# Attention kernel on one core: second weight halves, batch 1's normalisation and the last outputs in another order and on other engines

## The chip, the cores and the metric

The kernel runs on one core of a Trainium2 chip. The time is device microseconds (us) of the whole program on that core; it ran three times: 1285.94, 1286.47 and 1288.19 us, median 1286.47. Five engines work side by side, each through its own list of instructions in order: TensorE (PE; its weight loads are PEld), VectorE (DVE), ScalarE (ACT), GpSimd (POOL) and SyncE (SP, which issues the transfers). They wait for one another on semaphores.

## The reference

```python
def _layernorm(x, axis=-1, eps=1e-05):
    m = jnp.mean(x, axis=axis, keepdims=True)
    v = jnp.var(x, axis=axis, keepdims=True)
    return (x - m) / jnp.sqrt(v + eps)
# x: (32, 256, 512), adj: (32, 256, 256), W*: (512, 512), float32; 16 heads, hd = 32
h = jnp.maximum(_layernorm(x, axis=-1), 0.0)
q = split_heads(h @ Wq.T); k = split_heads(h @ Wk.T); v = split_heads(h @ Wv.T)
a = jnp.einsum('bhnd,bhmd->bhnm', q, k) * D ** (-0.5) + (adj + adj)[:, None]
row_nonzero = jnp.any(a != 0, axis=-1, keepdims=True)
a = jnp.where(row_nonzero, a, -jnp.inf)
p = jax.nn.softmax(a, axis=-1)
p = jnp.where(jnp.isnan(p), 0.0, p)
o = jnp.einsum('bhnm,bhmd->bhnd', p, v)
return x + o.transpose(0, 2, 1, 3).reshape(B, N, D) @ Wo.T
```

## The kernel before

Nearly every matrix is split into a high and a low part, so that a float32 product is made of three products (high by high, high by low, low by high) into one PSUM bank. A value is split in two steps: ACT copies it from PSUM into the high part, then DVE subtracts that from PSUM and writes the low part.

**Weights.** Wq, Wk and Wv arrive as six halves in the order `TURNS` (Wq 0, Wk 0, Wq 1, Wk 1, Wv 0, Wv 1). Of each half: its extent (DVE `weight_extent`, or ACT `sum_weight`), three small DVE instructions that make a scale (`weight_scales`), a multiplication by it in place (ACT for Wq 0, `scale_first_weight`; POOL for the other five, `scale_weight`, L929), eight transposes on PE (`turn`, L431), and the split (`high_weight` on ACT, `low_weight` on DVE). Half 0 of Wq and Wk is all that the products qk 0 and qk 1 (heads 0 to 7) read; half 1 serves qk 2 and qk 3.

**A batch.** POOL's `normalise` (L863) writes h from x and the moments that DVE's `moments_of` made; PE transposes it (job h); jobs qk and v are its products with the weights; SP restacks the parts of q and k for the scores by twelve transfers for each eight heads (`stack`, L242). Then for each of 16 heads: `scores` on PE, `shift` on DVE (adds 2 adj, takes the bound of each row), `exponentials` on ACT, `transpose_probs` on PE, `high_probs` on ACT and `low_probs` on DVE, `values` on PE. For each pair of heads POOL folds the rows to see whether one is all zero (`fold`), DVE makes the row factors (`any_nonzero`, `factors`), ACT copies the sums out of PSUM (`copy_outputs`) and POOL adds their halves and multiplies by the factors (`divide`, L884). Job o transposes eight heads' outputs, job y multiplies them by Wo, ACT copies y out of PSUM and POOL adds x (`residual`, L898).

**What sets the order.** A table, `JOBS`, says which pieces of which job PE does in which head's slot, and for which batch (-1, 0 or 1 from the present one). `body(b, first, last)` writes out one batch on each engine; batches 1 to 30 are a hardware loop, 0 and 31 are written out apart. Ahead of body 0 stand the instructions of the weights and of batch 0's first products; behind body 31 those that finish its outputs: `values` of heads 14 and 15, job o 1 (heads 8 to 15 together, into the bank `s_ps0`), and the second halves of y 0 and y 1 (L496 to L500). Their first halves stand in the slot of head 15, by `LAST_JOBS`, so ahead of the values of heads 14 and 15.

Of the kernel before, what the change touches and what calls it, by code (L numbers as in the profile page):

```python
# [47 lines left out]
LAST_JOBS = {15: [("y", 0, 0, 0, 6), ("y", 1, 0, 0, 6)]}  # L48


# [11 lines left out]
def jobs_at(hh, first, last):  # L62

    here = [j for j in JOBS[hh] if not (first and j[2] < 0) and not (last and j[2] > 0)]
    return here + (LAST_JOBS.get(hh, []) if last else [])

# [10 lines left out]
def attention_block(nc, x, adj, wq, wk, wv, wo_t, out):  # L77
# [23 lines left out]
    with ExitStack() as ctx:  # L101
# [102 lines left out]
        o_copied, y_ready = sem("o_copied"), sem("y_ready")  # L204
        stored = [sem(f"stored{i}") for i in range(NT)]
# [14 lines left out]
        def bank(kind, n, b):  # L220
# [4 lines left out]
            if isinstance(b, int) and (kind, n, b) == ("o", 1, B - 1):  # L225
                return 2
# [14 lines left out]
        def _(sp):  # L241
# [65 lines left out]
            for t in range(NT):  # L307
                store(B - 1, t)
# [4 lines left out]
        def _(pe):  # L313
# [140 lines left out]
            turn(WQ, 1)  # L454
# [40 lines left out]
            body(B - 1, False, True)  # L495
            for hh in range(HEADS - 2, HEADS):  # L496
                values(B - 1, hh, False)
            job("o", 1, -1, 0, 4, B)
            for n in range(NT):
                job("y", n, -1, 6, 12, B)  # L500

        @block.scalar
        def _(act):
# [105 lines left out]
            sum_weight(WQ, 1)  # L609
# [4 lines left out]
            high_weight(WQ, 1)  # L614
# [5 lines left out]
            high_weight(WK, 1)  # L620
            high_weight(WV, 0)
            high_weight(WV, 1)
            copy_adj(0)
            take("v", 0, 0, True)
            exponentials(0, 0, True)
# [28 lines left out]
            copy_outputs(B - 1, PAIRS - 1, False)  # L654
            take("o", 1, B - 1)
            for n in range(NT):
                take("y", n, B - 1)

        @block.vector
        def _(dve):  # L660
# [144 lines left out]
            weight_scales(WQ, 1)  # L805
            weight_scales(WK, 1)
# [12 lines left out]
            low_weight(WK, 1)  # L819
            low_weight(WV, 0)  # L820
            low_weight(WV, 1)
            take("v", 0, 0)
            shift(0, 0, True)
            take("qk", 2, 0)
            shift(0, 1, True)
# [29 lines left out]
        def _(pool):  # L855
# [93 lines left out]
            for half in range(2):  # L949
                scale_out_weight(half)  # L950
# [55 lines left out]
```

## Time and profile before

| | us |
|---|---|
| median of three runs | 1286.47 |
| the profiled execution, whole | 1286.69 |
| its span, first to last instruction | 1284.9 |
| PE busy in the span | 1246.0 (97%) |
| DVE busy | 1111.5 (87%) |
| ACT busy | 1052.2 (82%) |
| POOL busy | 898.3 (70%) |

The profile divides the span into busy time of each engine; a busy PE is not PE at its peak. Times in rows count from the span's start. The `<-` in brackets at the end of a row names what ended the engine's idle time before it.

### The profile page before, as it was taken

The page shows a single profiled execution, that of the slowest core. Times are in us where ns is not written, and L with a number is a line of the kernel's source. Part 1 is how long each engine was busy: PE and PEld are TensorE (multiplying, and loading weights), DVE is VectorE, ACT ScalarE, POOL GpSimd, SP SyncE. Part 2 cuts the span into 40 slices and gives each one's busy share as a digit, 9 for nine tenths or more (in the row PEclk, how much of TensorE's full clock was granted, in tenths as well). Part 3 has the DMA queues.
Part 4 walks back from the last instruction along what each step waited for, and adds up shares of the span by engine and source line. Part 5 has one row for each costly group of instructions (what it writes and reads, how often), then busy time and mean ns, then how long its engine had stood idle before and what let it go on. Part 6 is the DMA issues. An engine that isn't in the chain of part 4 may idle for free. (4 is left out here: it accounts for less than half of the span.)

```text
span 1284.9 us, 43970 instructions
## 1 busy us (share of the span) xinstructions
PE 1246.0 (97%) x13104; PEld 1110.2 (86%) x13104; DVE 1111.5 (87%) x4003; ACT 1052.2 (82%) x2429; POOL 898.3 (70%) x1272
## 2 busy tenths in 40 slices
PE   4899999999999999999999999999999999999996
PEld 4788988888988888888888888888888888988885
DVE  5798888888888888888888888888889898889884
ACT  4788888888888888888888888888888888888884
POOL 6676677776677776677776677776677776677765
PEclk9999999999999999999999999999999999999998
DMA  6344554554554554554554554554554554554551
GB/s 216 96 110 126 135 123 126 135 143 112 137 122 124 137 140 113 139 122 122 139 134 117 141 122 120 141 132 116 144 122 117 144 131 115 147 122 115 130 123 51
DMA packets 90772, 163.88 MB, mean 128 GB/s; under 512 B 14976, under 2 KB 23168, under 8 KB 90752
## 3 DMA queue, kind: packets, MB, share of 16 engines
q1 hardware_dynamic: 90752, 163.64, 49.1%
q8 instruction: 10, 0.16, 0.1%
q14 instruction: 10, 0.08, 0.0%
HBM read 46.14 MB, written 16.78 MB: 49 GB/s over the span
## 5 line engine op out<-in xcount | busy, mean ns | idle before, releaser
L912 POOL TENSOR_TENSOR fold<-minus 128x512 f32<-128x512 f32 x256 | 326.9, 1277 | 299.2 <-DVE bounds L765 299.2
L586 ACT ACTIVATE probs<-minus,bounds 128x256 f32<-128x256 f32 x1024 | 459.8, 499 | 26.6 <-DVE bounds L765 25.0
L774 DVE TENSOR_TENSOR pT_lo<-pT_ps,pT_hi 128x512 f16<-128x512 f32 x512 | 351.2, 686 | 63.2 <-ACT pT_hi L597 60.0
L765 DVE CUSTOM_DVE_ANT_0 minus<-s_ps,adj_now 128x256 f32<-128x256 f32 x1024 | 388.6, 416 | 7.7 <-ACT probs L586 4.7
L597 ACT ACTIVATE pT_hi<-pT_ps 128x512 f16<-128x512 f32 x512 | 304.9, 596 | 109.6 <-PE pT_ps L406 107.9
L406 PE MATMUL pT_ps<-ident,probs 128*128 128x128 f32 x2048 | 307.5, 273 | 1.7 <-ACT probs L586 1.6
L331 PE MATMUL job_ps<-hT_hi,w_hi 128*128 128x256 f16 x1024 | 280.5, 274 | 0.8 <-DVE hT_lo L729 0.8
L331 PE MATMUL job_ps<-hT_hi,w_lo 128*128 128x256 f16 x1024 | 279.2, 273 | 0.0
L331 PE MATMUL job_ps<-hT_lo,w_hi 128*128 128x256 f16 x1024 | 279.1, 273 | 0.0
L406 PEld LDWEIGHTS pT_ps<-ident,probs 128*128 128x128 f32 x2048 | 241.8, 141 | 19.0 <-ACT probs L586 2.5
L395 PE MATMUL s_ps<-qk_stack 96*128 96x256 f32 x1024 | 246.8, 323 | 0.0
L918 POOL TENSOR_TENSOR bounds<-fold 128x256 f32<-128x256 f32 x256 | 187.8, 734 | 24.9 <-POOL fold L912 9.5
L427 PE MATMUL o_ps<-v_parts,pT_hi 128*128 128x65 f16 x2048 | 157.1, 192 | 8.2 <-DVE pT_lo L774 7.7
L395 PEld LDWEIGHTS s_ps<-qk_stack 96*128 96x128 f32 x1024 | 154.6, 191 | 0.3 <-DMA qk_stack<-qk_parts 0.2
L428 PE MATMUL o_ps<-v_parts,pT_lo 128*128 128x33 f16 x2048 | 150.2, 178 | 0.0
L427 PEld LDWEIGHTS o_ps<-v_parts,pT_hi 128*128 128x128 f16 x2048 | 123.8, 97 | 24.0 <-DVE pT_lo L774 11.6
L331 PE MATMUL job_ps<-w_hi,hT_hi 128*128 128x256 f16 x512 | 140.7, 275 | 1.8 <-DVE qk_parts L737 1.8
L331 PE MATMUL job_ps<-w_lo,hT_hi 128*128 128x256 f16 x512 | 139.8, 273 | 0.0
L331 PE MATMUL job_ps<-w_hi,hT_lo 128*128 128x256 f16 x512 | 139.6, 273 | 0.0
L428 PEld LDWEIGHTS o_ps<-v_parts,pT_lo 128*128 128x128 f16 x2048 | 126.8, 96 | 0.0
L892 POOL TENSOR_TENSOR o<-o_raw,factor 128x128 f32<-128x128 f32 x256 | 103.1, 403 | 20.1
L331 PEld LDWEIGHTS job_ps<-hT_hi,w_hi 128*128 128x128 f16 x1024 | 99.8, 97 | 16.0 <-issue 0.9
(79 smaller groups left out, 2264.3 us busy)
## 6 DMA issues: line engine op xcount, KB each, us to landing
qk_stack<-qk_parts SPq DMA_DIRECT2D x768, 128.0 KB, 2.3
x_in<-x SPq DMA_DIRECT2D x32, 512.0 KB, 3.4
x_res<-x SPq DMA_DIRECT2D x32, 512.0 KB, 3.7
out<-y SPq DMA_DIRECT2D x64, 256.0 KB, 2.1
adj_in<-adj SPq DMA_DIRECT2D x32, 256.0 KB, 3.5
w_in<-wq SPq DMA_DIRECT2D x2, 512.0 KB, 6.1
w_in<-wk SPq DMA_DIRECT2D x2, 512.0 KB, 7.9
w_in<-wv SPq DMA_DIRECT2D x2, 512.0 KB, 9.9
```

What stands on the lines that cost most here:

```text
L331: end = nc.tensor.matmul(dst, lhs[a](k), rhs[c](k), start=i == 0, stop=i == len(terms) - 1)
L395: end = nc.tensor.matmul(s_ps[SCORE_BANK[hh]][:, t * N:(t + 1) * N], stack[:, 0, t * P:(t + 1) * P], stack[:, 1, :], start=True, stop=True)
L406: end = nc.tensor.transpose(pT_ps[hh % 2][:, m * N + t * P:m * N + (t + 1) * P], probs[hh % 2][:, t, m * P:(m + 1) * P], ident[:, :])
L427: nc.tensor.matmul(ps[:, 0:LOW + HD], hi, v[:, 0:LOW + HD], start=m == 0, stop=False)
L428: end = nc.tensor.matmul(ps[:, 0:HD + 1], lo, v[:, 0:HD + 1], start=False, stop=m == NT - 1)
L586: end = nc.scalar.activation(probs[hh % 2][:, t, :], minus[hh // 2 % 2][:, hh % 2, t, :], ACT.Exp, bias=bounds[:, hh // 2 % 4, 2 * (hh % 2 ...
L597: nc.scalar.activation(pT_hi[hh % 4][:, :, :], pT_ps[hh % 2][:, :].rearrange("p (m n) -> p m n", m=NT), ACT.Copy).then_inc(pT_high, 1)
L765: end = nc.vector.tensor_tensor_reduce(out=minus[pair % 2][:, hh % 2, t, :], in0=s_ps[SCORE_BANK[hh]][:, t * N:(t + 1) * N], in1=adj_now[: ...
L774: nc.vector.tensor_tensor(pT_lo[hh % 4][:, :, :], pT_ps[hh % 2][:, :].rearrange("p (m n) -> p m n", m=NT), pT_hi[hh % 4][:, :, :], ALU.sub ...
L892: nc.gpsimd.tensor_tensor(o[:, :, col:col + 2 * HD].rearrange("p t (h d) -> p h t d", h=2), o_raw[pair % 2][:, :, 0:HD].rearrange("p (h t) ...
L912: nc.gpsimd.tensor_tensor(f1[:, :, :], src[:, :, 0:N // 2], src[:, :, N // 2:N], ALU.add).then_inc(folded1, 1)
L918: nc.gpsimd.tensor_tensor(f2, f1[:, :, 0:N // 4], f1[:, :, N // 4:N // 2], ALU.add).then_inc(folded2, 1)
```

## The change

**Ahead of body 0.** PE does qk 0 and qk 1 before it turns Wq 1; Wk 1, Wv 0 and Wv 1 follow. ACT sums Wq 1 only after it has made the high part of Wk 0, and ACT and DVE split the four second halves after qk 1 is taken. The score products of heads 0 and 1 move one job forward. The multiplication of the weights on POOL gets a second operand, 1.0, with a second multiplication. DVE makes the moments of batch 1 and POOL normalises it there, and body 0 no longer does.

**Behind body 31.** `LAST_JOBS` goes. Heads 8 to 11 (k = 2) are transposed and split by themselves right behind head 15's transposes, heads 12 to 15 (k = 3) at the end; PE takes y in pieces of six, three and three products with the values of heads 14 and 15 after the first six. The last pair's sums are copied, added and multiplied by DVE, not by ACT and POOL, and the last residual is one DVE addition out of PSUM in place of an ACT copy and a POOL addition. The loop of batches 1 to 30 keeps its instructions.

```diff
-LAST_JOBS = {15: [("y", 0, 0, 0, 6), ("y", 1, 0, 0, 6)]}
@@ PE, ahead of body 0
             turn(WK, 0)
-            turn(WQ, 1)
             weight_waits(pe, WQ, 0)
             job("qk", 0, 0, 0, 12, 0)
             weight_waits(pe, WK, 0)
             job("qk", 0, 0, 12, 24, 0)
             job("qk", 1, 0, 0, 24, 0)
+            turn(WQ, 1)
             turn(WK, 1)
             turn(WV, 0)
             turn(WV, 1)
             weight_waits(pe, WV, 0)
+            scores(0, 0, True)
             job("v", 0, 0, 0, 12, 0)
-            scores(0, 0, True)
+            scores(0, 1, True)
             job("qk", 2, 0, 0, 24, 0)
-            scores(0, 1, True)
             job("v", 1, 0, 0, 12, 0)
@@ PE, behind body 31
+            def last_turn(k):
+                if k == 2:
+                    pe.wait_ge(o_ready, (B - 1) * PAIRS + 6)
+                else:
+                    pe.wait_ge(o_ready, (B - 1) * PAIRS + 7)
+                    pe.wait_ge(last_o, 1)
+                for t in range(NT):
+                    end = nc.tensor.transpose(s_ps[0][:, (k % 2) * N + t * P:(k % 2) * N + (t + 1) * P],
+                                              o[:, t, k * P:(k + 1) * P], ident[:, :])
+                end.then_inc(last_turned, 1)
...
+            last_turn(2)
+            last_product(0, 0, 6)
             for hh in range(HEADS - 2, HEADS):
                 values(B - 1, hh, False)
-            job("o", 1, -1, 0, 4, B)
-            for n in range(NT):
-                job("y", n, -1, 6, 12, B)
+            last_product(1, 0, 6)
+            last_product(0, 6, 9)
+            last_turn(3)
+            last_product(1, 6, 9)
+            last_product(0, 9, 12)
+            last_product(1, 9, 12)
@@ ACT, ahead of body 0
             scale_first_weight()
-            sum_weight(WQ, 1)
             high_weight(WQ, 0)
             for n in range(2):
                 take("h", n, 0)
             high_weight(WK, 0)
-            high_weight(WQ, 1)
+            sum_weight(WQ, 1)
             sum_weight(WV, 0)
@@ ACT, behind body 31
-            copy_outputs(B - 1, PAIRS - 1, False)
-            take("o", 1, B - 1)
-            for n in range(NT):
-                take("y", n, B - 1)
+            for k in range(2, KT):
+                act.wait_ge(last_turned, k - 1)
+                nc.scalar.activation(oT_hi[:, k, :], s_ps[0][:, (k % 2) * N:(k % 2 + 1) * N], ACT.Copy
+                                     ).then_inc(last_high, 1)
@@ DVE, ahead of body 0
             weight_extent(WK, 1)
-            weight_scales(WQ, 1)
-            weight_scales(WK, 1)
             low_weight(WQ, 0)
             for n in range(2):
                 take("h", n, 0)
             low_weight(WK, 0)
-            dve.wait_ge(w_scales, 4)
-            for half in range(2):
-                query_scales(half)
-            low_weight(WQ, 1)
+            dve.wait_ge(w_scales, 2)
+            query_scales(0)
+            weight_scales(WQ, 1)
+            weight_scales(WK, 1)
             take("qk", 0, 0)
...
+            shift(0, 0, True)
             take("v", 0, 0)
-            shift(0, 0, True)
+            shift(0, 1, True)
+            moments_of(1)
             take("qk", 2, 0)
-            shift(0, 1, True)
@@ DVE, behind body 31
+                dve.wait_ge(o_ready, (B - 1) * PAIRS + pair - 1)
+                nc.vector.tensor_copy(o_raw[pair % 2][:, :, 0:HD], o_sums[:, :, 0:HD]).then_inc(last_added, 1)
+                dve.wait_ge(last_added, 1)
+                nc.vector.tensor_tensor(o_raw[pair % 2][:, :, 0:HD], o_sums[:, :, LOW:LOW + HD],
+                                        o_raw[pair % 2][:, :, 0:HD], ALU.add).then_inc(last_added, 1)
...
+                nc.vector.tensor_tensor(y[:, t, :], job_ps[BANK["y", t]][:, :], x_res[:, t, :], ALU.add
+                                        ).then_inc(last_y, 1)
...
+            last_low(2)
+            last_outputs()
+            last_low(3)
+            for t in range(NT):
+                last_residual(t)
@@ POOL
                     end = nc.gpsimd.tensor_scalar(w_in[i][:, k, :], w_in[i][:, k, :],
-                                                  w_scale[:, i, UNSCALE, k:k + 1], None, ALU.mult)
+                                                  w_scale[:, i, UNSCALE, k:k + 1], 1.0, ALU.mult, ALU.mult)
...
+            normalise(1, False)
             fold(0, 0, True)
...
-                    if not last and hh == 1:
+                    if not (first or last) and hh == 1:
                         normalise(b + 1, False)
...
-            divide(B - 1, PAIRS - 1)
-            for t in range(NT):
-                residual(B - 1, t)
```

The order of PE ahead of body 0, before (w_in0, 1 and 2 are Wq, Wk and Wv; job_ps1 with w_hi0 is qk 0; s_ps2 and o_ps with w_in0 are the second half of Wq):

```order
L444 MATMUL s_ps0<-ident,w_in1 128x128 x4
L444 MATMUL s_ps1<-ident,w_in1 128x128 x4
L444 MATMUL s_ps2<-ident,w_in0 128x128 x4
L444 MATMUL o_ps<-ident,w_in0 128x128 x4
L331 MATMUL job_ps1<-hT_hi,w_hi0 128x256
L331 MATMUL job_ps1<-hT_lo,w_hi0 128x256
```

and after:

```order
L442 MATMUL s_ps0<-ident,w_in1 128x128 x4
L442 MATMUL s_ps1<-ident,w_in1 128x128 x4
L329 MATMUL job_ps1<-hT_hi,w_hi0 128x256
L329 MATMUL job_ps1<-hT_lo,w_hi0 128x256
...
L329 MATMUL job_ps0<-hT_hi,w_lo1 128x256
L442 MATMUL s_ps2<-ident,w_in0 128x128 x4
L442 MATMUL o_ps<-ident,w_in0 128x128 x4
L442 MATMUL pT_ps0<-ident,w_in1 128x128 x4
```

The eight transposes of Wq's second half have moved from ahead of the first product to behind the 48th. The last rows of DVE, before (pT_lo3 is head 15's low part, some and factor belong to the last pairs):

```order
L774 TENSOR_TENSOR pT_lo3<-pT_ps1,pT_hi3 128x512
L783 TENSOR_REDUCE some1<-bounds 128x4
L787 RECIPROCAL o_ps<-o_ps 128x4
L796 SCALAR_TENSOR_TENSOR factor1<-some1,o_ps 128x4
L747 TENSOR_TENSOR oT_lo<-s_ps0,oT_hi 128x512
```

and after:

```order
L803 TENSOR_TENSOR pT_lo3<-pT_ps1,pT_hi3 128x512
L882 TENSOR_TENSOR oT_lo<-s_ps0,oT_hi 128x256
L890 TENSOR_REDUCE some1<-bounds 128x4
L894 RECIPROCAL o_ps<-o_ps 128x4
L825 SCALAR_TENSOR_TENSOR factor1<-some1,o_ps 128x4
L898 COPY o_raw1<-o_ps 128x4x32
L900 TENSOR_TENSOR o_raw1<-o_ps,o_raw1 128x4x32
L905 TENSOR_TENSOR o<-o_raw1,factor1 128x2x2x32
L882 TENSOR_TENSOR oT_lo<-s_ps0,oT_hi 128x256
L917 TENSOR_TENSOR y<-job_ps1,x_res 128x512
L917 TENSOR_TENSOR y<-job_ps0,x_res 128x512
```

The split of the last transposed outputs has become two halves, and the pair's outputs and both residuals now stand on DVE.

## Rows read from the trace of the kernel before

**Rows 1.** Busy time by stretch: start:end, length, busy of each engine, PEclk, DMA, GB/s.

```profile
24.80:40.60 15.80, 10.37 (x79) 8.81 (x76) 7.25 (x20) 7.34 (x16) 9.27 (x9) 0.89 0.49 117
40.70:60.00 19.30, 16.30 (x175) 14.40 (x174) 16.36 (x60) 15.62 (x37) 14.75 (x19) 1.00 0.45 110
77.00:1263.00 1186.00, 1177.11 (x12509) 1051.30 (x12508) 1052.44 (x3815) 997.16 (x2306) 840.21 (x1199) 1.00 0.50 127
1273.00:1279.20 6.20, 4.79 (x13) 3.58 (x13) 0.69 (x1) 1.19 (x2) 0.18 (x1) 0.50 0.00 0
```

**Rows 2.** Timeline to 20 us: start, length, engine, line, operation, count, idle before.

```profile
11.50 1.22 DVE L677 TENSOR_REDUCE w_scale<-w_in 128x2 f32<-128x1024 f32 x1 [0.79 <-DMA w_in<-wk]
14.72 1.26 DVE L715 TENSOR_TENSOR w_lo<-pT_ps,w_hi 128x512 f16<-128x512 f32 x2
15.91 1.28 DVE L729 SCALAR_TENSOR_TENSOR hT_lo<-job_ps,hT_hi 128x512 f16<-128x512 f32 x2
17.06 1.11 PE L444 MATMUL s_ps<-ident,w_in 128*128 128x128 f32 x4 [1.99 <-POOL w_in L933]
18.82 0.42 PE L331 MATMUL job_ps<-hT_hi,w_hi 128*128 128x256 f16 x1
```

**Rows 3.** POOL's multiplications of weights, by line: ns min/median/max, first and last start.

```profile
L933 POOL TENSOR_SCALAR w_in<-w_in,w_scale x10: 1560/1563/1570, 10.8 to 29.1; 128x512 f32<-128x512 f32 x10
L942 POOL TENSOR_SCALAR wo_in<-wo_in,w_scale x4: 691/692/695, 30.7 to 32.7; 128x512 f32<-128x512 f32 x4
```

**Rows 4.** Timeline, 24 to 40 us.

```profile
24.65 1.04 PE L444 MATMUL pT_ps<-ident,w_in 128*128 128x128 f32 x8
26.03 0.41 DVE L737 SCALAR_TENSOR_TENSOR qk_parts<-job_ps,qk_parts 128x256 fp32r<-128x256 f32 x1
26.53 9.16 SPq L253 DMA_DIRECT2D qk_stack<-qk_parts  x12
30.70 1.12 PE L444 MATMUL s_ps<-ident,w_in 128*128 128x128 f32 x4 [1.99 <-POOL w_in L933]
34.61 0.28 PE L331 MATMUL job_ps<-hT_hi,w_hi 128*128 128x256 f16 x1
37.16 0.48 PE L395 MATMUL s_ps<-qk_stack 96*128 96x256 f32 x2
39.15 0.28 PE L331 MATMUL job_ps<-w_hi,hT_hi 128*128 128x256 f16 x1 [1.51 <-DVE qk_parts L737]
```

**Rows 5.** Transfers by line: count, KB each, median us from issue to landing.

```profile
qk_stack<-qk_parts SPq DMA_DIRECT2D x768, 128.0 KB, 2.3
x_in<-x SPq DMA_DIRECT2D x32, 512.0 KB, 3.4
out<-y SPq DMA_DIRECT2D x64, 256.0 KB, 2.1
```

**Rows 6.** Timeline, body 0 (from 40.7 us).

```profile
43.13 1.27 DVE L665 BATCH_NORM_STATS2 stats<-x_in 128x6 f32<-128x512 f32 x2
45.57 0.91 ACT L586 ACTIVATE probs<-minus,bounds 128x256 f32<-128x256 f32 x2 [1.62 <-PE pT_ps L406]
```

**Rows 7.** Timeline of the end.

```profile
1267.33 0.48 PE L331 MATMUL job_ps<-wo_hi,oT_hi 128*128 128x512 f32 x1 [0.26 <-DVE oT_lo L747]
1268.38 0.68 DVE L774 TENSOR_TENSOR pT_lo<-pT_ps,pT_hi 128x512 f16<-128x512 f32 x1
1270.21 0.20 PE L427 MATMUL o_ps<-v_parts,pT_hi 128*128 128x65 f16 x1
1270.85 0.39 ACT L575 ACTIVATE o_raw<-o_ps 128x260 f32<-128x260 f32 x1 [3.13 <-PE o_ps L428]
1272.73 1.11 PE L371 MATMUL s_ps<-ident,o 128*128 128x128 f32 x4 [1.92 <-POOL o L892]
1275.26 0.79 PE L331 MATMUL job_ps<-wo_hi,oT_hi 128*128 128x512 f32 x1 [1.41 <-DVE oT_lo L747]
1281.02 1.26 POOL L904 TENSOR_TENSOR y<-y,x_res 128x512 f32<-128x512 f32 x1 [0.72 <-ACT y L567]
```

More of the change, by code:

```diff
@@ L62, in jobs_at @@
 def jobs_at(hh, first, last):
-    here = [j for j in JOBS[hh] if not (first and j[2] < 0) and not (last and j[2] > 0)]
-    return here + (LAST_JOBS.get(hh, []) if last else [])
+    return [j for j in JOBS[hh] if not (first and j[2] < 0) and not (last and j[2] > 0)]
 def ended_before(hh, first, last):
@@ L224, in bank @@
                 return 1 - BANK[kind, n]
-            if isinstance(b, int) and (kind, n, b) == ("o", 1, B - 1):
-                return 2
             return BANK[kind, n]
@@ L619, in _ @@
             take("qk", 1, 0, True)
-            high_weight(WK, 1)
-            high_weight(WV, 0)
-            high_weight(WV, 1)
+            for i, half in TURNS[2:]:
+                high_weight(i, half)
             copy_adj(0)
+            exponentials(0, 0, True)
             take("v", 0, 0, True)
-            exponentials(0, 0, True)
             act.wait_ge(q_scales, 2)
@@ L842, in body @@
                     low_probs(b, hh, first and hh < 2)
-                    if not last and hh == 0:
+                    if not (first or last) and hh == 0:
                         moments_of(b + 1)
@@ L849, in _, with last_low, last_outputs @@
             body(B - 1, False, True)
-            any_nonzero(B - 1, PAIRS - 1)
-            factors(B - 1, PAIRS - 1, False)
-            take("o", 1, B - 1)
+            def last_low(k):
+                dve.wait_ge(last_high, k - 1)
+                nc.vector.tensor_tensor(oT_lo[:, k, :], s_ps[0][:, (k % 2) * N:(k % 2 + 1) * N],
+                                        oT_hi[:, k, :].bitcast(F32), ALU.subtract).then_inc(last_taken, 1)
+            def last_outputs():
+                pair = PAIRS - 1
+                dve.wait_ge(folded2, B * PAIRS)
+                nc.vector.tensor_reduce(some[pair % 2][:, :], bounds[:, pair % 4, :, :], AX_X, ALU.max,
+                                        apply_absolute_value=True).then_inc(some_ready, 1)
+                dve.wait_ge(pv_done, B * HEADS)
+                nc.vector.reciprocal(o_sums[:, :, FREE], o_sums[:, :, ONES]).then_inc(rcp_ready, 1)
+                factors(B - 1, pair, False)
+                dve.wait_ge(o_ready, (B - 1) * PAIRS + pair - 1)
[3 more added lines that the diff above has]
+                                        o_raw[pair % 2][:, :, 0:HD], ALU.add).then_inc(last_added, 1)
+                dve.wait_ge(last_added, 2)
+                dve.wait_ge(factor_ready, B * PAIRS)
+                col = 2 * pair * HD
+                nc.vector.tensor_tensor(
+                    o[:, :, col:col + 2 * HD].rearrange("p t (h d) -> p h t d", h=2),
+                    o_raw[pair % 2][:, :, 0:HD].rearrange("p (h t) d -> p h t d", h=2),
+                    factor[pair % 2][:, :].rearrange("p (h t) -> p h t", h=2).unsqueeze(3).to_broadcast([P, 2, NT, HD]),
+                    ALU.mult).then_inc(last_o, 1)
```

29 lines of the change are left out of this document (25 added, 4 removed).

## The prediction

> **What bounds the kernel now.** I read the busy time by stretch first. From 77 to 1263 us PE is busy for 1177.1 of 1186.0 us at a granted clock of 1.00 [rows 1]: 8.9 us of waiting in some 31 batches. The loop is bound by PE and its instructions do not change, so a microsecond won ahead of it moves the whole loop, and one won behind it moves the end. The same view shows where PE is not the bound: 10.4 busy of 15.8 us before body 0, 16.3 of 19.3 us in the first half of body 0, and 4.8 of 6.2 us at clock 0.50 near the end [rows 1]. So I work out three stretches from the timelines: to the first product of v 1, body 0, and the end.
>
> **Up to v 1.** Before, two things hold back the first product (18.82 us). PE stands in the turn of Wq 1, which waits 1.99 us for POOL at 17.06; and DVE, free at 11.50 + 1.22 = 12.72, makes the scales of Wq 1 and Wk 1 until it splits Wq 0 at 14.72 [rows 2]. Both go. ACT's high part of Wq 0 comes earlier too, because its sum of Wq 1 stands behind it now. So DVE's splits move up by 14.72 - 12.7 = 2.0 us, the low part of h ends at 15.91 + 1.28 - 2.0 = 15.2 us, and PE, which has nothing ahead, starts there: 3.6 us earlier. The second twelve products need Wk 0 split, a 1.26 us pair on DVE behind h, so at 16.4; the first twelve last until 16.5. It just fits.
>
> The 48 products of qk 0 and 1 took 24.65 - 18.82 = 5.8 us, the first at 0.42 us each [rows 2, 4]. Twenty-four at full level take 37.16 - 34.61 = 2.55 us [rows 4], so 48 take 5.1. PE will have been busier just before, so I let them run at full level: qk 1 ends at 20.4 instead of 24.65. DVE's take of it ended at 26.03 + 0.41 = 26.44 and the stacking of heads 0 to 7 began at 26.53 [rows 4]; both move up 4.2, to 22.3.
>
> From there DVE splits four second halves, 1.28 us each: Wq 1 by 23.6, Wk 1, then Wv 0 by 26.2, Wv 1 by 27.4. PE turns them at 1.04 to 1.1 us each from 20.4; the turn of Wv 1 uses the bank of Wq 1 and waits for its split, so ends at 24.8, and PE idles for 1.4 us until Wv 0 is split. This is the wait that comes in place of POOL's.
>
> POOL must not be later. Its ten multiplications of weights took 1563 ns each; the four of Wo, of the same 128x512 shape but with two operands and two multiplications, took 692 [rows 3]. The new form is the second one, so I price it at 0.69: Wq 1 can start when its scales are made (about 17.1 us, behind the query scales on DVE), the eight multiplications last 8 x 0.69 = 5.5 us, and with the wait for the scales of Wv they end near 23, ahead of PE's turn. The unknown lies between 0.69 and 1.56 by the rows; I take the lower because the instruction is the same as Wo's. The Trainium skill (GPSIMD Engine Reference, Elementwise, side-by-side cycle accounting) speaks against any gain here: up to two operations per element a body is bound by its ports, so a second multiplication should be free but not negative. The rows have it otherwise, 1563 against 692 ns, and the page's own example of 512 elements, 769 ns, lies by the two-operand rows. By the page read strictly both forms cost the same, and that case is the second rival.
>
> The scores of head 0 need three transfers and those of head 1 six. Twelve issues took 9.16 us, 0.76 each, and one lands in 2.3 us [rows 4, 5]: 22.3 + 1.5 + 2.3 = 26.1 and 22.3 + 3.8 + 2.3 = 28.4. PE: scores 0 at 26.2, v 0 until 27.9, scores 1 at 28.4, qk 2 from 28.7. In the kernel before qk 2 began at 34.61 and v 1, which waits for its bank, at 39.15 [rows 4]; the same 4.5 us give 33.2. DVE has more ahead of that take than before: the shifts of heads 0 and 1 and the moments of batch 1 (1.27 us of statistics and the aggregation [rows 6]), from 27.4 to about 32.3, then 0.9 for the take: also 33.2. Hence v 1 starts at 33.2 instead of 39.15, **5.9 us**. Bounds: 4.3 if the clock is at half level in the first products (+0.7) and in v 0 (+0.9); 6.6 if the waits for transfers and moments vanish.
>
> **Body 0.** DVE's moments stand at 43.13 ahead of head 3's shift, and ACT then waits 1.62 us at 45.57 [rows 6], from where on it is the engine that keeps PE waiting: PE's idle time from 40.7 to 60 us is 19.3 - 16.3 = 3.0 us [rows 1]. With the moments gone ACT is up to 1.6 us ahead. POOL loses its normalisation here and does it ahead of fold 0; the folds wait for DVE anyway. I take **1.2 us**: most of 1.62, less what PE's own work does not give back. Bounds 0 (PE cannot follow) and 3.0 (all its idle time).
>
> **The end.** Head 15's transposes and the first six products of y 0 keep their time (1267.33): two transposes of heads 8 to 11 slip in ahead while PE waits 0.26 us for DVE [rows 7]. Before, twelve products stood until 1270.21 ahead of the values of heads 14 and 15, whose last input was ready at 1268.38 + 0.68 = 1269.06 [rows 7]. Twelve took 2.88 us, so 0.24 each. After: six until 1268.8, the values until 1269.35, six of y 1 until 1270.8, three of y 0 until 1271.5. DVE meanwhile: half of oT low (128x256, 0.41 as in [rows 4]) until 1269.5; reduction, reciprocal and factor, each no larger than that, 0.7 together; copy, addition and multiplication of 128x128. Those three have no row before. From 0.68 for 512 columns and 0.41 for 256 I extrapolate 0.27, with hand-over 0.32 each; bounds 0 and 0.41. The output is ready at 1271.1, in time for the turn at 1271.5; there is 0.4 us to spare, so even 0.41 each costs nothing. Two transposes (0.3), ACT's copy (0.39), DVE's split (0.41) with their hand-overs end at 1272.8, beside three products of y 1 (until 1272.4). PE waits 0.4 us, does the last six products until 1274.35, and DVE's second residual (128x512, 0.68) ends at 1275.1.
>
> Before, the last addition ended at 1281.02 + 1.26 = 1282.28 and the span at 1284.9, 2.6 later. After, the two stores are issued 0.7 us apart instead of 2; 512 KB take 3.4 us against 2.1 for 256 KB [rows 5], so the second can be late by 0 to 0.7; I take 0.3. End at 1275.1 + 2.6 + 0.3 = 1278.0: **6.9 us** won. What went: ACT's copy (0.39) between values and factors, four transposes at 1.11 us and twelve products begun behind a wait, the first 0.79 us long against 0.48 [rows 7], and a 1.26 us addition behind an ACT copy. Bounds: 5.4 (last six products at half level, 0.2 more each, and the store's 0.7), 7.3 (nothing lost).
>
> **Sum.** 5.9 + 1.2 + 6.9 = 14.0. The profiled execution took 1286.69, of which 1284.9 is span; 1286.69 - 14.0 = 1272.7, and as it was 0.2 above the median of the runs shown, I predict 1272.5.
>
> **Rivals.** First, the clock. PE now has waits of 1.3 to 1.7 us at about 14, 25 and 31 us and 0.4 near the end. Before, a wait of 1.99 us was followed by four transposes in 1.11 us, against eight in 1.04 at full level [rows 2, 4], and the stretch to 40.6 us has clock 0.89 [rows 1]. If the shorter waits do the same, 0.7 + 0.9 in front and 6 x 0.2 = 1.2 at the end are lost: 1275.3. Against it: each is shorter than every wait after which the rows show half level. The Trainium skill (TensorE: Matmul & The Clock Gate, What's actually happening) has the throttled level as the default which activity lifts; that agrees with the 0.50 stretch, and it names no gap as short as these.
>
> Second, POOL's form costs 1.56 as before. Then eight multiplications from 17.1 end at 29.6, the turn of Wv 1 is at 29.7 instead of 30.70, and two pairs of scores now stand ahead of qk 2 (0.3 us more): v 1 comes 0.8 earlier, not 5.9. Sum 8.9: 1277.6. Only rows 3 speak against it, strongly.
>
> Third, slower: the loop settles in another rhythm. Ahead of it ACT, DVE and POOL come out of body 0 with other leads over PE. In body 0 that leads to 3.0 us of PE waits in half a batch. If a tenth of this stayed in each of 31 loop batches, 0.6 us each, 18.6 us are lost: 1291.1. It decides from 14.0 / 31 = 0.45 us a batch. Against it: the instructions and semaphores of the loop are the same, and before, PE's waits fell to 0.3 us a batch straight after a far more disturbed body 0.
>
> Fourth, the gains are absorbed: transfers or DVE hold v 1 where it was and the end gains little; within 0.2%, about 1286.
>
> **Numbers.** Forecast 0.78, clock 0.10, POOL's form 0.08, rhythm 0.02, absorbed 0.02. Runs of this kernel can tell 0.2% (2.6 us) from no change; so faster 0.96, same 0.02, slower 0.02. The range goes from the sum of the high bounds, cut where they would all have to hold together (1269.0), to just past the second rival (1278.0).
>
> **What would show it.** POOL's weight multiplications at about 0.69 us; the first qk product near 15.2, the first stacking transfer near 22.3, the first product of v 1 near 33.2; ACT's 1.6 us wait in body 0 gone; as much time in the loop as before, with PE waiting under 10 us in it; at the end, PE at full level with one wait of about 0.4 us and 2.6 to 3.3 us from the last addition to the end. The prediction is wrong if those multiplications stay at 1.56, if clock 0.50 appears before 33 us or in the last 6 us, or if PE's waits in the loop rise by more than a few us.

## The result and the profile after

The changed kernel took 1275.87 us (median of five runs, 1272.42 to 1277.27), the kernel before beside it 1286.22 us (five runs, 1285.45 to 1288.19): ratio 0.9914, interval 0.9902 to 0.9927. It is faster, by 10.4 us in the medians, and the median lies in the range that was forecast (1269.0 to 1278.0). The profiled execution took 1273.81 us with a span of 1272.0; against the 1286.69 of the one before that is 12.9 us, where the steps of the prediction made 14.0.

GpSimd's multiplications, by line (ns min/median/max, first and last start), of the kernel after, beside [rows 3]:

```profile
L1005 POOL TENSOR_SCALAR w_in<-w_in,w_scale x10: 691/692/704, 10.4 to 22.0; 128x512 f32<-128x512 f32 x10
```

The new form costs what the two-operand form of Wo cost. Now the timeline ahead of v 1 of the kernel after (start, length, engine, line; in brackets the idle time before it and what ended it), beside [rows 2, 4]. Read PE's five rows with a bracket first: they are its waits.

```profile
14.91 0.27 PE L329 MATMUL job_ps<-hT_hi,w_hi 128*128 128x256 f16 x1 [1.54 <-DVE hT_lo L758]
...
18.58 0.48 DVE L764 SCALAR_TENSOR_TENSOR qk_parts<-job_ps,q_scale,qk_parts 128x256 fp32r<-128x256 f32 x1 [1.45 <-ACT qk_parts L583]
...
22.04 8.63 SPq L249 DMA_DIRECT2D qk_stack<-qk_parts  x12
...
23.85 0.63 PE L442 MATMUL s_ps<-ident,w_in 128*128 128x128 f32 x4 [0.91 <-DVE w_lo L744]
...
26.15 0.80 PE L393 MATMUL s_ps<-qk_stack 96*128 96x256 f32 x2 [1.23 <-DVE w_lo L744]
...
26.98 0.42 PE L329 MATMUL job_ps<-w_lo,hT_hi 128*128 128x256 f16 x1
...
29.55 0.28 PE L329 MATMUL job_ps<-hT_hi,w_hi 128*128 128x256 f16 x1
...
34.10 0.28 PE L329 MATMUL job_ps<-w_hi,hT_hi 128*128 128x256 f16 x1 [1.75 <-DVE qk_parts L766]
```

Product v 1 starts at 34.10 us, 5.05 us earlier than before. From 26.15 us PE runs at half level: the two scores take 0.80 us, and each product of v 0 takes 0.42 us where the others take 0.27. The busy time by stretch (columns as in rows 1) shows it as a granted clock of 0.66 in 25 to 30 us, after waits of 1.54, 0.91 and 1.23 us, and shows the loop as it was:

```profile
25.00:30.00 5.00, 3.85 (x20) 3.00 (x21) 3.11 (x9) 2.84 (x6) 0.34 (x1) 0.66 0.74 170
71.00:1257.00 1186.00, 1177.02 (x12507) 1051.16 (x12505) 1052.32 (x3814) 996.75 (x2305) 839.71 (x1199) 1.00 0.50 127
```

PE is busy for 1177.02 us of 1186, against 1177.11 [rows 1]. ACT copies adj once in every batch, so these copies are marks in the loop. One mark near its start and the last mark, first of the kernel before and then of the kernel after:

```profile
L606 ACT ACTIVATE adj_now<-adj_in x2: 633/634/634, 110.1 to 148.7; 128x512 f32<-128x512 f32 x2
L606 ACT ACTIVATE adj_now<-adj_in x1: 633/633/633, 1230.0 to 1230.0; 128x512 f32<-128x512 f32 x1
```

```profile
L636 ACT ACTIVATE adj_now<-adj_in x2: 633/633/633, 103.8 to 142.5; 128x512 f32<-128x512 f32 x2
L636 ACT ACTIVATE adj_now<-adj_in x1: 633/633/633, 1224.2 to 1224.2; 128x512 f32<-128x512 f32 x1
```

From 148.7 to 1230.0 it was 1081.3 us, from 142.5 to 1224.2 it is 1081.7. The 6.2 us won by the first mark are 5.05 up to v 1 and 1.2 in body 0, as PE's first product of qk 0 of batch 1 shows, first in the kernel before and then in the kernel after:

```profile
57.06 0.27 PE L331 MATMUL job_ps<-hT_hi,w_hi 128*128 128x256 f16 x1 [0.82 <-DVE hT_lo L729]
```

```profile
50.82 0.27 PE L329 MATMUL job_ps<-hT_hi,w_hi 128*128 128x256 f16 x1 [0.81 <-DVE hT_lo L758]
```

From v 1 to there it was 17.9 us and is 16.7. ACT's wait ahead of `probs` [rows 6] is gone: it came 6.42 us behind v 1, and the same instruction now starts 4.69 us behind v 1, without a bracket.

```profile
38.79 0.90 ACT L616 ACTIVATE probs<-minus,bounds 128x256 f32<-128x256 f32 x2
```

The profile names PE as what ended the old wait. PE's transposes and DVE's shift of head 3 ended there within 0.01 us of each other; that it was the shift shows in the kernel after, where the instruction starts ahead of those transposes.

The end of the kernel after, beside [rows 7]:

```profile
1260.60 0.63 PE L404 MATMUL pT_ps<-ident,probs 128*128 128x128 f32 x4
...
1264.80 0.29 DVE L905 TENSOR_TENSOR o<-o_raw,factor 128x128 f32<-128x128 f32 x1
...
1265.70 0.38 PE L503 MATMUL s_ps<-ident,o 128*128 128x128 f32 x2
...
1267.01 0.50 PE L329 MATMUL job_ps<-wo_hi,oT_hi 128*128 128x512 f32 x1 [0.23 <-DVE oT_lo L882]
...
1267.58 0.39 PE L329 MATMUL job_ps<-wo_hi,oT_lo 128*128 128x512 f32 x1
...
1268.11 1.36 DVE L917 TENSOR_TENSOR y<-job_ps,x_res 128x512 f32<-128x512 f32 x2 [1.15 <-PE job_ps L329]
```

The clock stays at full level (0.39 us a product, where the half-level one in rows 7 took 0.79 with its start). PE has one wait, 0.23 us. From the transposes of head 15 (1260.60) to the end of the span it is 11.4 us; before, where they stand in this row, it was 18.5.

```profile
1266.43 0.64 PE L406 MATMUL pT_ps<-ident,probs 128*128 128x128 f32 x4
```

### The profile page after: what moved, and what is told of

Read it like the earlier page. It is cut to its first block and busy times, and to the rows that moved or that the text cites. A ratio compares the mean times of both kernels' runs of the same rounds, so it can differ in the third digit from the quotient of the medians.

```text
span 1272.0 us, 43970 instructions
## 1 busy us (share of the span) xinstructions
PE 1241.6 (98%) x13104; PEld 1107.2 (87%) x13104; DVE 1112.8 (87%) x4009; ACT 1050.6 (83%) x2427; POOL 886.1 (70%) x1268
## 5 line engine op out<-in xcount | busy, mean ns | idle before, releaser
L329 PEld LDWEIGHTS job_ps<-hT_hi,w_hi 128*128 128x128 f16 x1024 | 99.7, 97 | 17.6 <-issue 2.6
```

Of the source, the lines that this page charges most:

```text
L329: end = nc.tensor.matmul(dst, lhs[a](k), rhs[c](k), start=i == 0, stop=i == len(terms) - 1)
```

## The experiments

Every kernel was timed four or five times, in three sets (1 to 4, 5 to 8, 9 to 12), each with the kernel before beside it. I call the distance between the lowest and the highest run of a kernel its scatter; much of the story hangs on it. The kernel before scatters too: by 4.2, 4.3 and 2.7 us in the nine runs of each set. The code below is shortened; `...` marks what is left out.

**1 and 2. The front alone, the end alone.** The first has everything ahead of body 0 and the old end; the second the reverse.

```diff
@@ e1: the kernel before with
+ front of every engine, the form with 1.0, moments_of(1) and normalise(1) ahead
@@ e2: the kernel before with
+ last_turn, last_product, last_low, last_outputs, last_residual; no LAST_JOBS
```

> The part ahead of body 0 and the moved normalisation alone, the end as before. Theory A (the gains add, each where the prediction put it): 6.2 us off the kernel before (5.05 by the first product of v 1, 1.2 in body 0), so near 1280.0, and in the trace v 1 at 34.1 us. Theory B (what the loop does with its start takes part of it back, the 2 us by which the median of the changed kernel lies above its profiled execution): 4 us off, near 1282.2, with the loop longer by 2 us and v 1 still at 34.1.

> The new end alone, everything ahead of the loop and body 0 as before. Theory A: 7.1 us off the kernel before, near 1279.1, with TensorE at full level to the end. Theory B gives the same 7.1, since the start is the old one. If it is the end that varies between executions (TensorE's level there), the times scatter by 1 to 2 us and the mean gain is 5.5.

Measured: 1280.32 us (1279.77 to 1280.42, ratio 0.9954, interval 0.9940 to 0.9967) and 1279.20 us (1277.46 to 1280.31, ratio 0.9947, interval 0.9933 to 0.9961), before 1285.89. The front is worth 5.6 us and the end 6.7, each by an interval of some 3.5 us in width. Together 12.3; the whole change was worth 11.8 in the same set (next run). The parts add up within what the runs can tell, and the loop took the same: from mark to mark, as above, 1081.5 us in the first and 1081.7 in the second. In the front-only kernel v 0 ran at half level again, and there PE had waited only 0.81, 0.91 and 1.23 us:

```profile
25.00:30.00 5.00, 3.77 (x21) 2.75 (x20) 3.59 (x10) 2.89 (x6) 0.76 (x2) 0.70 0.91 207
```

Two things in these traces warn against trusting one pair of profiles. In the end-only kernel the front is that of the kernel before, and still v 1 comes 2.46 us earlier than in the profile of before:

```profile
36.69 0.28 PE L329 MATMUL job_ps<-w_hi,hT_hi 128*128 128x256 f16 x1 [1.51 <-DVE qk_parts L768]
```

And in the front-only kernel the old end, from the transposes of head 15 (1260.81) to the end of the span (1278.4), took 17.6 us, not 18.5. So by the traces the new end is worth 6.2 to 7.1 us.

**3. The changed kernel again.** No edit.

> The changed kernel once more, unaltered, for a second profile and five more times. If its scatter (1272.4 to 1277.3) is a scatter of TensorE's level, the span follows the granted clock: about 1.3 us more for each 0.001 less (1275 us x 0.001 at half speed cost 1275 x 0.001 = 1.3 us), and the median lies between 1273 and 1276.5. If it is the loop whatever the clock, spans differ at equal clock.

Measured: 1274.08 us (1273.87 to 1275.95), ratio 0.9909, interval 0.9895 to 0.9923. In this execution the half level stood elsewhere: PE waited 1.95 us ahead of the first product, and some fifteen of the 24 products of qk 0, from 16.05 us on, took 0.42 us each; v 0 ran at full level.

```profile
15.61 0.27 PE L329 MATMUL job_ps<-hT_hi,w_hi 128*128 128x256 f16 x1 [1.95 <-DVE hT_lo L758]
...
35.10 0.28 PE L329 MATMUL job_ps<-w_hi,hT_hi 128*128 128x256 f16 x1 [1.89 <-DVE qk_parts L766]
```

```profile
15.00:18.00 3.00, 2.39 (x14) 1.81 (x15) 2.65 (x10) 2.22 (x8) 0.57 (x1) 0.67 1.04 387
25.00:30.00 5.00, 2.86 (x24) 2.25 (x23) 5.00 (x11) 3.23 (x7) 2.72 (x5) 1.00 0.79 179
```

v 1 came a microsecond later than in the other trace. The same kernel has more than one front. As to what was expected of the scatter: the clock is not all of it. Four of these five runs show the same mean granted clock, 0.999, with spans from 1272.1 to 1274.1 us, and the one at 0.998 lies between them, at 1272.9.

**4 and 5. PE's waits filled with products that nobody reads.** The first fills the wait at 25 us, the second also those ahead of the first product and of v 1.

```diff
@@ e4, e5: PE, behind the turn of Wv 1
+            pe.wait_ge(taken["qk"], 1)
+            for _ in range(11):
+                nc.tensor.matmul(job_ps[BANK["qk", 2]][:, 0:N], w_hi[WQ][:, 0, 0:P], hT_hi[:, 0, :],
+                                 start=True, stop=True)
@@ e5 alone: ahead of qk 0
+            for _ in range(10):
+                nc.tensor.transpose(o_ps[:, 0:P], ident[:, :], ident[:, :])
@@ e5 alone: ahead of v 1
+            pe.wait_ge(taken["v"], 1)
+            for _ in range(14):
+                nc.tensor.matmul(job_ps[BANK["qk", 3]][:, 0:N], w_hi[WQ][:, 0, 0:P], hT_hi[:, 0, :],
+                                 start=True, stop=True)
```

> The changed kernel with eleven products of 256 columns, whose results are overwritten, in TensorE's wait of 1.2 us ahead of head 0's scores. Theory A with the clock as the missing 0.9 us: TensorE stays at full level from 25 to 30 us, the twelve products of v 0 take 1.3 us instead of 2.4, v 1 starts at 33.2 to 33.4 instead of 34.10, 0.8 us faster than the changed kernel. Rival: the level falls whatever fills that wait, or DVE's moments hold v 1 anyway: no change within 0.2 us in the trace.

> The changed kernel with work for TensorE in all three of its waits ahead of body 0: ten transposes of the unit matrix at about 13.4 us, the eleven products at 25 us, and fourteen products ahead of v 1; all their results are overwritten. Theory C (the scatter of the changed kernel, and what its median lies above the prediction, is TensorE's half level after one of these waits): every execution at full level, so median 1272.0 to 1273.0 with a narrow scatter of 1 us, the rest being the arrival of the first weights. Rival D (the scatter is the arrival of the weights alone): the same scatter of 2 to 3 us and the median of the changed kernel, 1274 to 1276.

Measured: 1273.27 us (1272.51 to 1275.65, ratio 0.9904, interval 0.9889 to 0.9918) and 1273.10 us (1272.71 to 1273.84, ratio 0.9901, interval 0.9886 to 0.9916). With one wait filled v 1 starts here:

```profile
32.85 0.28 PE L329 MATMUL job_ps<-w_hi,hT_hi 128*128 128x256 f16 x1 [1.75 <-DVE qk_parts L770]
```

PE in the second, with the waits filled at 13.65, 24.85 and 30.95 us, and its clock:

```profile
24.85 1.36 PE L465 MATMUL job_ps<-hT_hi,w_hi 128*128 128x256 f16 x11
...
30.95 1.69 PE L474 MATMUL job_ps<-hT_hi,w_hi 128*128 128x256 f16 x14
...
32.86 0.28 PE L329 MATMUL job_ps<-w_hi,hT_hi 128*128 128x256 f16 x1 [0.22 <-DVE qk_parts L776]
```

```profile
25.00:30.00 5.00, 4.96 (x44) 4.05 (x42) 3.76 (x10) 2.78 (x6) 0.62 (x1) 1.00 0.78 175
```

In both v 0 runs at full level and v 1 starts 1.2 us earlier (32.85 and 32.86 against 34.10); the wait at 25 us alone makes that difference. The mean granted clock is 1.0 in four of five runs of the first and in all four of the second, against one in ten of the changed kernel. So filling the waits takes the half level in front away; that a wait need not bring it, run 8 will show. The scatter of the second is 1.1 us, against 4.9 and 2.1 for the changed kernel's first and second five runs; that points to the half level as a large part of it, but with four runs, and with spans that differ at equal clock, it is not shown. The medians of the three kernels lie within what the runs can tell apart; the trace and the clock carry this, not the medians.

**6 and 7. The form of GpSimd's multiplication, in the new order and in the old.**

```diff
@@ e6: the changed kernel with
-                                                  w_scale[:, i, UNSCALE, k:k + 1], 1.0, ALU.mult, ALU.mult)
+                                                  w_scale[:, i, UNSCALE, k:k + 1], None, ALU.mult)
@@ e7: the kernel before with the reverse of it, and nothing else
```

> The changed kernel with GpSimd's multiplication of the weights in its old form, one operand (undone: 1.0 and the second multiplication). By the prediction's second rival: ten instructions of 1.56 us instead of 0.69, the last ends at 16.7 + 8 x 1.56 = 29.2 us, v 1 starts near 38.4 instead of 34.1, 4.3 us slower than the changed kernel: 1278 to 1280. Rival (order alone carries the gain in front, GpSimd has slack): v 1 near 34.5 and no loss.

> The kernel before with nothing changed but the form of GpSimd's multiplication of the weights (1.0 and a second multiplication added). If GpSimd is what held the old front: the first product at 17.3 us (held by VectorE's splits), the last turn at 25.8 instead of 30.7, v 1 near 34.5 to 35, 4 us faster than before: 1282. If the old order is what held it: 1.6 us faster, with v 1 at 37.5.

Measured: 1280.14 us (1279.61 to 1281.49, ratio 0.9955, interval 0.9941 to 0.9968) with the old form, 1279.55 us (1279.00 to 1280.59, ratio 0.9951, interval 0.9937 to 0.9965) with the new form alone. With the old form the new order has PE waiting three times for POOL behind qk 1, and v 1 comes at 40.14 us, a microsecond later than before the change. The first row is POOL's line in ns:

```profile
L1005 POOL TENSOR_SCALAR w_in<-w_in,w_scale x10: 1564/1570/1575, 10.4 to 28.7; 128x512 f32<-128x512 f32 x10
```

```profile
24.17 1.10 PE L442 MATMUL pT_ps<-ident,w_in 128*128 128x128 f32 x8 [1.98 <-POOL w_in L1005]
...
27.25 1.97 PE L442 MATMUL s_ps<-ident,w_in 128*128 128x128 f32 x8 [1.99 <-POOL w_in L1005]
...
30.34 1.12 PE L442 MATMUL s_ps<-ident,w_in 128*128 128x128 f32 x4 [1.11 <-POOL w_in L1005]
```

With the new form and everything else old, v 1 is there at 32.38 us, earlier than in the changed kernel:

```profile
12.62 2.77 PE L444 MATMUL s_ps<-ident,w_in 128*128 128x128 f32 x12
...
12.72 0.19 DVE L693 TENSOR_SCALAR w_scale<-w_scale 128x2 int32<-128x2 int32 x1
...
15.67 0.27 PE L331 MATMUL job_ps<-hT_hi,w_hi 128*128 128x256 f16 x1
...
17.28 0.69 DVE L715 TENSOR_TENSOR w_lo<-s_ps,w_hi 128x512 f16<-128x512 f32 x1
...
25.81 0.28 PE L331 MATMUL job_ps<-w_hi,hT_hi 128*128 128x256 f16 x1 [1.16 <-DVE w_lo L715]
...
27.83 0.28 PE L331 MATMUL job_ps<-hT_hi,w_hi 128*128 128x256 f16 x1
...
32.38 0.28 PE L331 MATMUL job_ps<-w_hi,hT_hi 128*128 128x256 f16 x1 [1.51 <-DVE qk_parts L737]
```

This run taught me most. I expected 4 us of the form alone and it gave 6.4: all of the front's gain. (By the traces it is 6.8 at v 1 against the profile of before, and 4.3 against the same front in run 2.) In the old order the turn of Wq 1, no longer kept waiting by POOL, fills the time in which PE must wait for h anyway (12.62), so the first product is only 0.76 us later than in the new order. It also gave back time on DVE: the six small instructions that make the scales of Wq 1 and Wk 1 took 2.1 us in the kernel before (12.63 to 14.72) and take 1.0 here (12.06 to 13.03). One of them in the kernel before, beside the row at 12.72 above:

```profile
13.98 0.63 DVE L693 TENSOR_SCALAR w_scale<-w_scale 128x2 int32<-128x2 int32 x1
```

DVE splits Wq 1 at 17.28, where in the changed kernel it stands idle for 1.45 us, and has three halves left behind qk 1 instead of four. v 0 begins at 25.81 at full level, the scores of head 1 don't stand ahead of qk 2, and qk 2 starts at 27.83 instead of 29.55.

**8. Batch 1's moments and normalisation back in body 0.**

```diff
@@ the changed kernel with
-            moments_of(1)
...
-                    if not (first or last) and hh == 0:
+                    if not last and hh == 0:
                         moments_of(b + 1)
...
-            normalise(1, False)
...
-                    if not (first or last) and hh == 1:
+                    if not last and hh == 1:
                         normalise(b + 1, False)
```

> The changed kernel with batch 1's moments and normalisation back in body 0. Prediction: ScalarE waits 1.6 us for head 3's shift again and TensorE comes to qk 0 of batch 1 1.2 us later counted from v 1; v 1 itself stays within 0.2 us, since VectorE's take of qk 2 waits for ScalarE and not for the moments. Rival: body 0 absorbs it, since ScalarE's later waits shrink, and the loss is under 0.4 us.

Measured: 1274.33 us (1272.83 to 1274.83), ratio 0.9907, interval 0.9894 to 0.9921: the same as the changed kernel. This profiled execution had no half level in front although its waits are those of the changed kernel, so v 1 came at 33.11 us; qk 0 of batch 1, the next place where every front has the same work behind it, came at 50.60 us, 17.5 later, where the changed kernel took 16.7. ACT waits for DVE again, at the place of the wait in [rows 6], but for 1.19 us:

```profile
39.10 0.91 ACT L616 ACTIVATE probs<-minus,bounds 128x256 f32<-128x256 f32 x2 [1.19 <-DVE bounds L794]
```

From v 1 on the move is worth 0.8 us in this order. Ahead of v 1 it costs 0.2 at full level: with the moments there (run 4) it is 18.06 us from the first product to v 1, without them 17.84. By the medians none of it can be told.

**9 and 10. The form and the end on the old order; and batch 1's moments ahead as well.** The second is what the earlier runs pointed to.

```diff
@@ e9: the kernel before with
+ 1.0, ALU.mult, ALU.mult in scale_weight, and the new end
@@ e10: e9 with
+            moments_of(1)          (DVE, between shift(0, 0) and the taking of qk 2)
+            normalise(1, False)    (POOL, ahead of fold(0, 0))
```

> The kernel before with two of the changed kernel's parts: the weight multiplications with 1.0 and a second multiplication, and the whole new end. The order of the front stays the old one, and batch 1's moments stay in body 0. Theory A (the front's gain is the form's alone, the new order adds nothing, and front and end add up): the kernel with the new form alone took 1279.55 us and the new end alone was worth 6.7 us, so 1272.7 us, 1.0 to 1.5 us below the changed kernel. In the trace product v 1 starts near 32.4 us, qk 0 of batch 1 near 50.3 us, and the end from the turn of head 15 takes 11.4 us as in the changed kernel. Theory B (the new order has a worth that showed only with the new end, or the good stretch of the form-only kernel's front was chance): not below the changed kernel, 1274 us or more, v 1 at 34 us or later.

> As the kernel before it in this row of runs (old order of the front, new form, new end), with batch 1's moments on VectorE between the first shift and the taking of qk 2, and its normalisation on GpSimd ahead of the first fold. Theory A (moving the moments shortens body 0 by what the traces showed: from v 1 to qk 0 of batch 1 it was 16.7 us in the changed kernel, 17.5 us with the moments back and 17.9 us in the old order): v 1 still near 32.4 us, qk 0 of batch 1 near 49.2 us, 1.1 us less than without it, so 1271.6 us, the fastest of all. Theory B (the moments lie on the way in this front, ahead of the taking of qk 2, for which VectorE had waited for ScalarE anyway): v 1 later by up to 1 us, and no difference, 1272.6 us.

Measured: 1273.22 us (1272.37 to 1273.60, ratio 0.9892, interval 0.9877 to 0.9907) and 1271.92 us (1271.66 to 1272.56, ratio 0.9883, interval 0.9868 to 0.9898), before 1286.55. The first product of v 1, ACT's wait in body 0 and the first product of qk 0 of batch 1, in the first, and v 1 and qk 0 in the second, where ACT does not wait for head 3's shift:

```profile
32.16 0.28 PE L329 MATMUL job_ps<-w_hi,hT_hi 128*128 128x256 f16 x1 [1.52 <-DVE qk_parts L768]
...
38.59 0.91 ACT L616 ACTIVATE probs<-minus,bounds 128x256 f32<-128x256 f32 x2 [1.64 <-DVE bounds L796]
...
50.09 0.27 PE L329 MATMUL job_ps<-hT_hi,w_hi 128*128 128x256 f16 x1 [0.82 <-DVE hT_lo L760]
```

```profile
32.20 0.28 PE L329 MATMUL job_ps<-w_hi,hT_hi 128*128 128x256 f16 x1 [1.52 <-DVE qk_parts L768]
...
48.92 0.27 PE L329 MATMUL job_ps<-hT_hi,w_hi 128*128 128x256 f16 x1 [0.81 <-DVE hT_lo L760]
```

v 1 stands still and qk 0 comes 1.17 us earlier; the medians say 1.3. The moments lie in DVE's wait of 2.6 us for ACT's part of qk 2 and cost nothing. The second of them is the fastest kernel of all, with a scatter of 0.9 us. The changed kernel itself was not timed in this set. Its nearest stand-in there is run 12, which has its front and, as shown below, an end of the same worth: 1273.67 us. All runs of the second kernel lie below all of that one's (highest 1272.56, lowest 1272.86), 1.75 us apart in the medians; the first kernel, at 1273.22, can't be told from it.

**11 and 12. The two halves of the VectorE part of the end, each undone.**

```diff
@@ e11: last residual
-                nc.vector.tensor_tensor(y[:, t, :], job_ps[BANK["y", t]][:, :], x_res[:, t, :], ALU.add)
+                nc.scalar.activation(y[:, t, :], job_ps[BANK["y", t]][:, :], ACT.Copy)
+                nc.gpsimd.tensor_tensor(y[:, t, :], y[:, t, :], x_res[:, t, :], ALU.add)
@@ e12: the last pair's outputs
-                last copy, addition and multiplication on DVE
+                copy_outputs(B - 1, PAIRS - 1, False) on ACT, divide(B - 1, PAIRS - 1) on POOL
```

> The changed kernel with the last residual as before: ScalarE copies each half of the last product (0.60 us), GpSimd adds x to it (1.28 us each). The rest of the end stays. From the trace of the changed kernel the last product ends near 1268.8 us; VectorE's two additions (0.68 us each) end at 1269.47 us. With the old pair the first addition would run 1268.7 to 1270.0 us and the second to 1271.3 us. Theory A (the stores start behind the additions and nothing hides them): 1.8 us more than the changed kernel, 1275.9 us against 1274.1 us. Theory B (the stores set the end, and the first of the two hides the second addition): under 0.8 us more.

> The changed kernel with the last pair's outputs as before: ScalarE copies the 128x260 sums (0.41 us), GpSimd adds the low parts and multiplies by the factor (0.41 us each), in place of VectorE's 0.28, 0.29 and 0.29 us. Theory A (the three steps stand in one chain to the last turn, and TensorE's products beside them end before they do, as its wait ahead of the last turn says): the turn of heads 14 and 15 starts 0.4 to 0.7 us later and the kernel takes 0.5 us more than the changed kernel, 1274.6 us against 1274.1 us. Theory B (the six products of the first half, which stand ahead of the turn, cover it): within 0.2 us of the changed kernel.

Measured: 1274.71 us (1274.55 to 1275.91, ratio 0.9904, interval 0.9889 to 0.9919) and 1273.67 us (1272.86 to 1277.08, ratio 0.9900, interval 0.9886 to 0.9914). The residual on ACT and POOL:

```profile
1267.33 0.50 PE L329 MATMUL job_ps<-wo_hi,oT_hi 128*128 128x512 f32 x1 [0.24 <-DVE oT_lo L886]
...
1268.38 1.30 ACT L690 ACTIVATE y<-job_ps 128x512 f32<-128x512 f32 x2 [1.57 <-PE job_ps L329]
...
1269.12 2.48 POOL L1055 TENSOR_TENSOR y<-y,x_res 128x512 f32<-128x512 f32 x2 [5.20 <-ACT y L690]
```

Its last six products start 0.32 us later than in the changed kernel (the front was that much longer), and its last addition ends at 1269.12 + 2.48 = 1271.60 instead of 1268.11 + 1.36 = 1269.47: 2.13, so 1.8 us are the residual's, as theory A has it. The medians show 0.6 against the changed kernel's second five runs, 1.0 against run 12 beside it, and the lowest runs 2.1 against the changed kernel's lowest of all: the scatter is too wide to price it by medians. The outputs on ACT and POOL:

```profile
1265.44 0.40 POOL L951 TENSOR_TENSOR o<-o_raw,factor 128x128 f32<-128x128 f32 x1
...
1266.00 0.38 PE L502 MATMUL s_ps<-ident,o 128*128 128x128 f32 x2
```

The turn starts without a wait, right behind the products, 0.16 us after POOL is done; in the changed kernel, where it starts as directly, DVE had been done since 1265.09, 0.6 us ahead. Theory B holds: this part of the change is worth nothing by itself, since PE's products cover both versions. Theory A's reading of PE's wait was wrong: that wait stands behind the turn, not ahead of it.

## Why the prediction was right, and where it was not

**Up to v 1: 5.9 forecast, 5.05 measured in the profiled execution.** The step that failed is the full level of v 0 ("scores 0 at 26.2, v 0 until 27.9"). "I let them run at full level" held for qk 0 and qk 1 in that execution. v 0 ran at half level, which I had at 0.9 us as a lower bound and as part of the first rival. It cost 1.2: with the wait ahead of it filled v 1 starts at 32.85 (run 4), 6.3 us earlier than before. My argument against that rival, that each new wait is shorter than any wait after which rows of before show half level, fell: half level in v 0 followed waits of 1.54, 0.91 and 1.23 us, and in run 1 waits of 0.81, 0.91 and 1.23. The rival had a tenth of my chances. In front it came true in all five traces of the new order with the new form, the moments ahead and PE's waits left unfilled, in v 0 in four of them and in qk 0 in the third run, at 1.2 of the 1.6 us that it had for the front in the profiled execution; in the last products, where I had put the rest of its price, it did not. The steps on the way stood: 0.69 us for GpSimd's form, first product at 14.91 (15.2), stacking at 22.04 (22.3). The 5.05 itself hangs on the profile of before: against the same old front in run 2 (v 1 at 36.69) it would be 2.6. The medians of run 1 give 5.6 for v 1 and body 0 together, where I had 7.1.

**What the 5.9 was made of.** Here the total was nearly right and its parts were not, and that it came out is in part luck. I worked the gain out of the new order, with the form only as what must not spoil it. The runs show the reverse: the form alone gives 6.4 us (run 7), while the whole front, form, order and moved moments together, gives 5.6 (run 1); the two can't be told apart. With the form, the moments ahead and the new end in both, the old order took 1271.92 us, the new one 1275.87, 1274.08 and, as run 12 beside it, 1273.67, and with its waits filled, so at full level, 1273.10. So the new order adds no gain to the form's and costs something. By the traces, at the first product of qk 0 of batch 1: 48.92 us in the old order, 49.59 in the new one at full level (runs 4 and 5), and 50.82 to 51.84 in its five traces with half level. That is 0.7 us in work and waits and 1.2 to 2.3 more in the traces with half level. Not all of the 2.3 need be the clock's, since the first product stands at 14.79 to 15.61 us in these traces. What I missed is visible in [rows 2, 4]: both 1.99 us waits of PE are waits for POOL's multiplication, and they would go with the form whatever the order. Of the 2.0 us by which I let DVE's splits move up because the scales go from ahead of them, 1.1 went with the form too (run 7).

**GpSimd's form as rival: 0.8 earlier forecast, 1.0 later measured.** In that case I gave PE one wait at the turn of Wv 1; it had three behind qk 1, with half level behind the second and the third and again in v 1. The median was 1280.1 against my 1277.6.

**Body 0: 1.2 forecast.** It is 1.2 in the changed kernel and 1.2 on the old order (runs 9 and 10), and 0.8 in the new order with the moments back. The mechanism is shown too: ACT's wait of 1.64 us cost PE 1.2, the one of 1.19 us cost 0.8, and with the moments ahead neither is there. In the new order 0.2 of it is paid back ahead of v 1 (run 8). In run 6, with v 1 at half level, the stretch was 18.4 us although the moments were ahead: the 1.2 holds for v 1 at full level.

**The loop: unchanged forecast, +0.4 us measured over 1081.** The same stretch took 1081.5 to 1081.8 us in the traces of runs 1, 2, 3, 8, 9 and 10, the old front of run 2 among them, so the 0.4 is not of the change. The slower rival is out.

**The end: 6.9 forecast, 7.1 measured.** PE's one wait is 0.23 us (0.4), the small DVE instructions 0.28 to 0.29 (0.27), and from the last addition to the end it is 2.5 us (2.6 to 3.3). Against the old end of run 1, which ran at half level for less long, it is 6.2, and the medians of run 2 give 6.7. Of the 7.1 the residual is 1.8 and the outputs on VectorE are 0. The rest, 4.4 to 5.3, I put down to the order of turns and products, with the full level that goes with it; no run takes these two apart.

**The sum.** 5.05 + 1.2 - 0.4 + 7.1 = 12.95, and the spans of the profiled executions differ by 12.9. The median of the changed kernel's first five runs lies 2.1 us above its own profiled execution; scatter of that size, in this kernel and in the one before, I had nowhere in the sum. The second five runs (run 3) put the gain at 11.8. That the slower executions had half level in more places than the traced one was not seen, only made likely by the filled kernel.

## What to carry to other kernels

When a change mixes a cheaper instruction with a new order, price the instruction first in the old order: the waits that the new order was to work around may all go with it. Work that lies in a wait which the engine has anyway is free; the turn of Wq 1 was, and moved out of that wait it no longer was. Look at the scatter of the runs, and at a second trace, before you explain one: here the same front differed by 2.5 us at one product. Traces with half level after this prologue's waits came 1.2 to 2.3 us later, and in the trace with one wait filled that was gone.

## What was not expected of the hardware

- GpSimd's multiplication of 128x512 float32 by a column takes 1563 to 1570 ns (medians of ten) with one operand and 691 to 697 ns with 1.0 and a second multiplication, in both orders of the program (the kernel before, run 6; run 7, the kernel after). The Trainium skill (GPSIMD Engine Reference, Elementwise, side-by-side cycle accounting) would have both cost the same; the measurement decides.
- Some of DVE's small instructions (128x2) take longer while GpSimd's one-operand multiplication runs: in the three traces with that form (before, runs 2 and 6) three of them take 0.38 to 0.63 us, in the eleven traces with the other form none of the same instructions takes over 0.34, and most take 0.15 to 0.19. The form is what these traces differ in; how it reaches DVE no run shows.
- Half level was not a fixed price of a wait. It followed PE's waits of 1.54, 0.91 and 1.23 us in one execution of the changed kernel, one of 1.95 us in another, and waits of 0.81, 0.91 and 1.23 us in run 1. The kernel of run 8 had waits of 1.85, 0.91 and 1.24 us there and kept full level, and so did the old order with the new form, with waits of up to 1.52 us. With all three waits filled every run had a granted clock of 1.0. What decides in between is open.
